# Second attention of a four-layer kernel: three SP transfers change place or queue, and the router's logits go in four parts

## The reference, cut to what matters

```
scores = einsum('bhqd,bhkd->bhqk', q, k) * scale, causal, + head_scales * geo
attn = softmax(scores);  out = einsum('bhqk,bhkd->bqhd', attn, v) @ w_out
x3 = layernorm(x2 + out)                 # x2: tokens before this layer
xn = rmsnorm(x3) * norm_weight
logits = xn @ router_weight.T + router_bias
probs = softmax(logits); gate_vals, expert_idx = top_k(probs, 2)
pos = rank of each choice within its expert; slot = min(pos, CAP - 1)
dispatch[e, slot] += xn;  experts run on dispatch;  results are gathered
```

## Time and profile before

| | us |
|---|---|
| time, median of 3 runs (1979.17 to 1983.17) | 1980.51 |
| time of the profiled execution | 1971.93 |
| its span | 1970.2 |
| mean granted clock | 0.945 |
| PE busy | 1813.4 (92%) |
| DVE busy | 1427.4 (72%) |
| ACT busy | 1123.9 (57%) |
| POOL busy | 504.8 (26%) |

### The profile page before, as it was taken

The page is one execution under the profiler, slowest core; times in us unless marked ns, Lnnn a source line. Parts: engine busy times, 40 slices in busy tenths (PEclk is TensorE's granted clock), DMA queues, the critical chain, the costliest instruction groups (busy, mean ns, idle before and its releaser), DMA issues. The chain is left out here.

```text
span 1970.2 us, 34757 instructions
## 1 busy us (share of the span) xinstructions
PE 1813.4 (92%) x12676; PEld 1183.6 (60%) x12676; DVE 1427.4 (72%) x2803; ACT 1123.9 (57%) x2228; POOL 504.8 (26%) x648
## 2 busy tenths in 40 slices
PE   8979999999999999799999889899897968899992
PEld 4545444444444444588888755555554457899992
DVE  7869999999999996467776465556564354566663
ACT  4635888888888889323222225454453523555554
POOL 5750000332000001222221122115142243244441
PEclk9976999999999999899999969989998989999996
DMA  4883734654354302115434466527463243556645
GB/s 168 289 239 46 116 82 93 142 137 127 62 82 71 63 19 81 41 51 176 138 107 128 153 164 145 127 65 192 99 168 85 72 160 109 134 142 146 157 91 184
DMA packets 169717, 238.99 MB, mean 121 GB/s; under 512 B 25689, under 2 KB 109178, under 8 KB 169568
## 3 DMA queue, kind: packets, MB, share of 16 engines
q1 hardware_dynamic: 138256, 178.82, 37.2%
q0 software_dynamic: 15200, 26.76, 5.8%
q10 hardware_dynamic: 16112, 31.46, 4.5%
HBM read 136.97 MB, written 96.60 MB: 119 GB/s over the span
## 5 line engine op out<-in xcount | busy, mean ns | idle before, releaser
L989 DVE TENSOR_REDUCE b_mx<-b_PM 128x1 f32<-128x512 f32 x1024 | 621.1, 681 | 22.3 <-PE b_PM L843 21.9
L965 ACT ACTIVATE b_probs<-b_PS 128x512 f32<-128x512 f32 x1000 | 523.9, 606 | 69.0 <-PE b_PS L897 53.7
L2784 ACT ACTIVATE d_probs<-d_PS 128x512 f32<-128x512 f32 (+3 forms) x384 | 167.0, 496 | 211.4 <-PE d_PS L2695 210.8
L843 PE MATMUL b_PM<-b_kst,b_qst 48*128 48x512 f32 x888 | 281.3, 431 | 0.0
L897 PE MATMUL b_PS<-b_qst,b_kst 50*128 50x512 f32 x744 | 256.8, 436 | 2.0 <-issue 0.2
L2824 DVE TENSOR_REDUCE d_mx<-d_PM 128x2 f32<-128x1024 f32 (+1 forms) x192 | 180.1, 950 | 97.4 <-PE d_PM L2647 66.0
L897 PEld LDWEIGHTS b_PS<-b_qst,b_kst 50*128 50x128 f32 x744 | 120.5, 184 | 163.3 <-ACT b_probs L965 147.5
L2747 POOL TENSOR_SCALAR_AFFINE_SELECT d_probs<-d_probs 128x128 f32<-128x128 f32 x256 | 73.8, 301 | 281.0 <-ACT d_probs L2784 276.4
L869 PE MATMUL b_PO<-b_probs,x_v 128*32 128x384 f32 (+2 forms) x2048 | 145.3, 390 | 0.0
L843 PEld LDWEIGHTS b_PM<-b_kst,b_qst 48*128 48x128 f32 x888 | 142.0, 184 | 5.1
L869 PE MATMUL b_PO<-b_probs,b_vst 128*32 128x384 f32 (+3 forms) x1960 | 143.0, 397 | 1.0 <-ACT b_probs L965 0.9
(11 more groups left out here) (300 smaller groups left out, 3762.4 us busy)
## 6 DMA issues: line engine op xcount, KB each, us to landing
halves<-a_parts SPq DMA_DIRECT2D x7, 2048.0 KB, 8.7
qk<-c_halves ACTq DMA_DIRECT2D x7, 2048.0 KB, 12.4
w_w<-L_ffn_fc1T SPq DMA_DIRECT2D x12, 1024.0 KB, 5.0
w_w<-L_ffn_fc2T SPq DMA_DIRECT2D x12, 1024.0 KB, 6.4
b_qst<-halves SPq DMA_DIRECT2D x72, 128.0 KB, 4.4
b_kst<-halves SPq DMA_DIRECT2D x72, 128.0 KB, 7.5
d_qst<-qk SPq DMA_DIRECT2D x36, 256.0 KB, 4.5
d_kst<-qk SPq DMA_DIRECT2D x36, 256.0 KB, 6.6
```

What stands on the lines that cost most here:

```text
L843: mm = pe.matmul(PM[n % MBANKS][:], qst[buf][at, p, first:first + P], kst[buf][at, p, kh * BLK:(kh + 1) * BLK], start=True, stop=True)
L965: act.activation(probs[:, s % RING], score_bank(g, s)[:], ACT.Exp).then_inc(exped, 1)
L989: dve.tensor_reduce(mx[:, half, (r * PAIRS0 + p) * TPH + t, kh:kh + 1], PM[n % MBANKS][:], AX.X, ALU.max)\
L2784: act.activation(probs[:, s % RING, 0:w], PS[bank(s)][:, 0:w], ACT.Exp).then_inc(exped, 1)
```

## The change

- `load_shares(g-1, 1)` stands ahead of `load(g+3)` on SP's queue instead of behind it. It does so in every group, so also in the first group of the next batch, which brings a batch's last shares.
- `load_tokens` and the `tokens.store` of batches 0 to 2 move from SP's queue to POOL's, to tick 4 of the same groups (T % 12 == 4, between POOL's masks of i = 3 and i = 8). POOL then waits for `x3_done` before it loads x2. The last two stores stay on SP and signal on a semaphore of their own.
- The logits of a full batch come in four parts of two token tiles each, at k = 27, 28, 29 and 30. Each part takes a place in the ring and has its own DVE scaling. The half batches at the end keep one part, at k = 30.
- All that follows the logits comes three ticks later: exponentials at 33, ranks at 42, scatter at 46 to 61. In the tail, where there is no attention, the order of the instructions stays the same.

```
-    LOGITS, EXPS, RANKS = 27, 30, 39
-    SCATTER = 43
+    LOGITS = (27, 28, 29, 30)
+    CHOICE = LOGITS[-1]
+    EXPS, RANKS = 33, 42
+    SCATTER = 46
...
+    def part_at(cls, u, k):
+        if k in cls.parts(u):
+            i, share = cls.parts(u).index(k), cls.UNITS[u][1] // len(cls.parts(u))
+            return i, range(i * share, (i + 1) * share), cls.parts_through(u - 1) + i + 1
...
             if b > 1:
-            sp.wait_ge(self.logits_ready, b - 1)
+            sp.wait_ge(self.logits_ready, self.parts_through(b - 2))
...
-    def load_tokens(self, sp, d, b):
+    def load_tokens(self, pool, d, b):
         if b > 0:
-            sp.wait_ge(self.x3_done, b * TPB)
+            pool.wait_ge(self.x3_done, b * TPB)
...
-        if k == self.LOGITS:
-            dve.wait_ge(self.logits_ready, u + 1)
+        if part := self.part_at(u, k):
+            i, ts, through = part
+            dve.wait_ge(self.logits_ready, through)
...
                 if g + 1 < GROUPS:
                     rows(g + 1)
+                if g > 0:
+                    route.load_shares(sp, d, g - 1, 1)
                 if g + BUFS - 1 < GROUPS:
                     if g > 0:
                         sp.wait_ge(pv_done, g * ROUNDS + RING // G1)
                     load(g + BUFS - 1)
-                if g > 0:
-                    route.load_shares(sp, d, g - 1, 1)
                 route.store_shares(sp, d, g, 0)
-                b = g // HG1
-                if g % HG1 == HG1 - 2:
-                    route.load_tokens(sp, d, b)
-                if g % HG1 == HG1 - 1 and b > 0:
-                    for n in range((b - 1) * HPS, b * HPS):
-                        tokens.store(sp, d, n)
...
+                if T < GROUPS * ROUNDS and T % ROUNDS == TPK:      # on POOL, behind mask(T)
+                    g = T // ROUNDS
+                    b = g // HG1
+                    if g % HG1 == HG1 - 2:
+                        route.load_tokens(pool, d, b)
+                    if g % HG1 == HG1 - 1 and b > 0:
+                        for n in range((b - 1) * HPS, b * HPS):
+                            tokens.store(pool, d, n, tokens.x3_out)
```

More of the change, by code:

```diff
@@ L1569, in __init__, with store @@
         self.x3 = a.sb("x3", [P, TILES, DIM])
-        self.x3_out = a.sem("x3_out")
+        self.x3_out, self.last_x3_out = a.sem("x3_out"), a.sem("last_x3_out")
         self.sums_in = [a.sem(f"sums_in{n}") for n in range(BLOCKS)]
-    def store(self, sp, d, n):
-        sp.dma_start(d["sums1"][n * BLK:(n + 1) * BLK, :].rearrange("(t p) c -> p t c", p=P),
-                     self.x3[:, n * TPK:(n + 1) * TPK]).then_inc(self.x3_out, 16)
+    def store(self, eng, d, n, out):
+        eng.dma_start(d["sums1"][n * BLK:(n + 1) * BLK, :].rearrange("(t p) c -> p t c", p=P),
+                      self.x3[:, n * TPK:(n + 1) * TPK]).then_inc(out, 16)
     def load_sums(self, sp, d, n):
@@ L1593 @@
     STEPS = 20
-    TICKS = 59
+    TICKS = 62
     WEIGH, WEIGH_LAST = (8, 12), (1,)
@@ L1610 @@
     LAST_POOL = dict(zip(range(SCATTER + BEHIND, SCATTER + BEHIND + 2 * TPK), zip(range(SCATTER, SCATTER + 2 * TPK))))
-    FILLS = {("project", 6): 26, ("project", 7): 24, ("logits", 3): 5, ("turn", 7): 8, ("logits", 4): 5}
+    FILLS = {("project", 6): 26, ("project", 7): 24, ("logits", 3, 0): 5, ("turn", 7): 8, ("logits", 4, 0): 5}
     LEAD = TPB // 2
@@ L1700, in entries, with parts, parts_through @@
     @classmethod
+    def parts(cls, u):
+        return cls.LOGITS if cls.UNITS[u][1] == TPB else cls.LOGITS[-1:]
+    @classmethod
+    def part_at(cls, u, k):
+        if k in cls.parts(u):
+            i, share = cls.parts(u).index(k), cls.UNITS[u][1] // len(cls.parts(u))
+            return i, range(i * share, (i + 1) * share), cls.parts_through(u - 1) + i + 1
+    @classmethod
+    def parts_through(cls, u):
+        return sum(len(cls.parts(i)) for i in range(u + 1))
+    @classmethod
     def entries(cls, u, k):
@@ L1706, in entries @@
                 found.append((name, n))
-        if k == cls.LOGITS:
-            found.append(("logits", u))
+        if part := cls.part_at(u, k):
+            found.append(("logits", u, part[0]))
         if k == cls.RANKS:
@@ L1772, in load_shares @@
         sp.dma_start(self.shares[b % 2][to % P:to % P + G1 * D1, half, to // P], share).then_inc(self.shares_in[half], 16)
-    def load_tokens(self, sp, d, b):
+    def load_tokens(self, pool, d, b):
         if b > 0:
-            sp.wait_ge(self.x3_done, b * TPB)
+            pool.wait_ge(self.x3_done, b * TPB)
         for i in range(HPS):
             tok = slice(b * SEQ + i * BLK, b * SEQ + (i + 1) * BLK)
-            sp.dma_start(self.x2[:, i], d["x2"][tok, :].rearrange("(t p) c -> p t c", p=P)).then_inc(self.x2_in[i], 16)
+            pool.dma_start(self.x2[:, i], d["x2"][tok, :].rearrange("(t p) c -> p t c", p=P)).then_inc(self.x2_in[i], 16)
     def wait_weights_free(self, sp, b):
         sp.wait_ge(self.projected, (b + 1) * HPS)
-        sp.wait_ge(self.logits_ready, b + 1 if b + 1 < BATCH else len(self.UNITS))
+        sp.wait_ge(self.logits_ready, self.parts_through(b if b + 1 < BATCH else len(self.UNITS) - 1))
     def fill(self, pe, ident, spare, *name):
@@ L1821, in multiply @@
             mm.then_inc(self.x3_turned, 1)
-        if k == self.LOGITS:
-            self.fill(pe, ident, spare, "logits", u)
-            out = self.bank("logits", u)
+        if part := self.part_at(u, k):
+            name = ("logits", u, part[0])
+            self.fill(pe, ident, spare, *name)
+            out = self.bank(*name)
             for n in self.blocks(u):
                 self.taken(pe, "turn", n)
-            self.free(pe, "logits", u)
-            for t in range(count):
+            self.free(pe, *name)
+            for t in part[1]:
                 i, at = (start + t) // TPK % HPS, (start + t) % TPK * P
@@ L1944, in choose @@
                .then_inc(self.xn_done, 1)
-        if k == self.LOGITS:
-            dve.wait_ge(self.logits_ready, u + 1)
[L1947 to L1950, removed]
+        if part := self.part_at(u, k):
+            i, ts, through = part
+            dve.wait_ge(self.logits_ready, through)
+            these = slice(lo + ts[0], lo + ts[-1] + 1)
+            dve.tensor_tensor(self.scaled[:, these],
+                              self.bank("logits", u, i)[:, 0, ts[0] * E:(ts[-1] + 1) * E].rearrange("p (t e) -> p t e", e=E),
+                              self.rroots[:, 1, these].unsqueeze(2).to_broadcast([P, len(ts), E]), ALU.mult)\
+               .then_inc(self.max_taken[self.entry["logits", u, i] % 2], 1)
+        if k == self.CHOICE + 1:
+            for i in range(len(self.parts(u))):
+                self.taken(dve, "logits", u, i)
             dve.tensor_tensor(self.logits[:, us], self.scaled[:, us], self.br[:].unsqueeze(1).to_broadcast([P, count, E]), ALU.add)\
@@ L1954, in choose @@
             dve.tensor_reduce(self.top[:, us], self.logits[:, us], AX.X, ALU.max).then_inc(step, 1)
-        if k == self.LOGITS + 2:
+        if k == self.CHOICE + 2:
             past(2)
@@ L1966, in choose @@
             dve.sem_inc(self.seen, 1)
-        for tile in self.tiles_at(u, k, self.LOGITS + 5):
+        for tile in self.tiles_at(u, k, self.CHOICE + 5):
             t = tile % TPB
@@ L1973, in choose @@
                 dve.sem_inc(self.seen, 1)
-        if k == self.LOGITS + 8:
+        if k == self.CHOICE + 8:
             for t in range(lo, lo + count // 2):
                 dve.max_index(self.besti[:, t], self.best[:, t], self.prob[:, t])
-        if k == self.LOGITS + 9:
+        if k == self.CHOICE + 9:
             for t in range(lo + count // 2, lo + count):
@@ L1984, in choose @@
         lead = self.SCAN_AT[u]
-        if k == self.LOGITS + 10:
+        if k == self.CHOICE + 10:
             past(9)
@@ L1993, in choose @@
                .then_inc(step, 1)
-        if k == self.LOGITS + 11:
+        if k == self.CHOICE + 11:
             for i in range(3):
@@ L2289, in gpsimd @@
         assert PLAIN * ST == MLPS
-        pool.wait_ge(tokens.x3_out, 16 * BLOCKS)
+        pool.wait_ge(tokens.x3_out, 16 * (BLOCKS - HPS))
+        pool.wait_ge(tokens.last_x3_out, 16 * HPS)
         for n in range(MLPS):
@@ L2623, in _ @@
                 sp.wait_ge(route.x3_done, (n + 1) * TPK)
-                tokens.store(sp, d, n)
+                tokens.store(sp, d, n, tokens.last_x3_out)
             route.wait_weights_free(sp, BATCH - 1)
```

4 lines of the change are left out of this document (2 added, 2 removed).

## The result

The changed kernel takes 1966.89 us (median of 9 runs, 1960.53 to 1970.71) against 1978.51 us (9 runs, 1974.21 to 1983.17) for the kernel before: ratio 0.9938, 95% interval 0.9922 to 0.9954. It is faster, by 12 us. The prediction said 1945.5 us, 35 us faster, with a range up to 1962. It had the sign and missed the size by a factor of three.

The account below looks back on a forecast made before the run. PE was taken to bound the second attention, with gains from its idle gaps and slow clock. 19.2 + 8.9 + 7.0 - 0.6 - 0.4 + 1.0 = 35 us, from the median of 1980.5 to 1945.5 us, with a range up to 1962.

Parts of the forecast that it names:

- the delay of the load behind the shares: SP's queue: the load comes one DMA issue of 0.58 us later, its buffers used more than a group later.
- Shares ahead of the load: Odd blocks' projections: three DVE waits go, 12.31 us, and the clock stays up, 6.91 us; together 19.2 us gained.
- Tokens on POOL: Waits for totals: PE gaps of 7.12 us and 4.2 us of slow clock go, less 2 x 1.20: 8.9 us gained.
- Logits: Logits in four parts: the slow clock behind units 0 and 2 goes; 7.0 us gained of at most 8.4.
- the banks: Logits: each part takes a bank, so the next tick's maximum waits for DVE; 0.2 us lost per unit, 0.6 in all.
- Choice three ticks later: DVE's small instructions meet other maxima and the ranks come to a short tick: a loss of 0.4 us in all.
- Tail: After x3 stores leave SP's queue the last shares can be earlier: between 0 and 2.2 us, taken as 1 gained.
- A: PE's clock falls elsewhere, behind small gaps or small products: 18 us not gained, 17 us faster, 1963.5 us; chance 0.12.
- B: Totals late all the same, token transfers sharing the 16 DMA engines: 8.9 us missing, 1954.5 us; chance 0.10.
- C: Token DMAs on POOL hold up the masks of round 8: 12 us slower at c = 8, 1992 us; chance 0.06.
- D: Shares land no earlier than DVE needs them because their own store lands late: 16 us left, 1964.5 us; chance 0.04.
- signs of being wrong: Batch periods between projections not falling some 12 us each, PEclk falling at new places, or DVE's wait for totals staying.

Follow-up runs that it names:

- the wide shares: Kernel before with its shares, still behind the large load, read by one DMA per head instead of one for two heads: 1961.92 us, ratio 0.9909.
- 15.3 in the second: The changed kernel run once more for a second profile, beside the kernel before at 1971.38 us: 1956.09 us, ratio 0.9921.
- the wide one: Changed kernel with the shares read by one DMA per head, run twice: 1936.51 us, ratio 0.9824, and 1956.26 us, ratio 0.9884.
- the wide kernel with later ranks: Changed kernel with shares by one DMA per head and ranks at k = 43 instead of 42: 1948.24 us, ratio 0.9842.
- the second and third series: Two series of four kernels, each on one chip beside the kernel before, at 1981.12 and 1979.43 us: ratios 0.9842 to 0.9946 and 0.9864 to 1.0002.
- the first series: Four kernels on one chip beside the kernel before at 1971.38 us: changed again, shares ahead in first groups only, wide shares, late weights; 0.9824 to 0.9921.

## Why the prediction missed the size

Two steps failed, the delay of the load behind the shares (put at nothing, 8.7 us) and the choice with its ranks (put at -0.4 us, measured -5.5). Both are read from the pair of traces.

*Shares ahead of the load.* The gain was forecast at 19.2 us and is 19.2 in this execution: the gaps at 1.33 to 1.47 us for 1.43, the projections at 3.72 us for 3.69. In several other executions with the shares in this place one or two of the three projections come at the slower clock (5.41 us), so it is in part luck that none did here. The first step that failed is the sentence behind it: "Behind the shares the load's eight instructions come one DMA issue of 0.58 us later; their buffers are used more than a group later." Both halves were wrong (and the instructions are seven). The load of group g + 3 goes out at about tick 8 of group g, and PE asks for its keys at tick 6 of group g + 1. In the trace after, `x_k` was issued from 1202.80 and PE stood for it until 1216.96, 14.2 us later. PE's wait began at 1214.33. Had each transfer landed in the 6.7 us of before, they would have been in time by some 4 us (by 4.8 for the first of the three, which are issued within a microsecond). That was all the slack. And the delay is not one issue but what the two-head DMA holds up behind it. This took 8.7 us in batch 0. No term of the sum asked what the shares' DMA costs by itself: its 10.66 us to land were read as "behind the load" alone. The trace of before had more to say. With no load ahead of it, the even half's DMA was issued at 1255.44 and DVE started on it at 1260.25, 4.8 us later, where a wide one lands in 2.1 us.

*Tokens on POOL.* 8.9 us forecast, 7.5 found here and 6.6 in the kernel with this part alone. The pair of direct DMAs was taken at 2 us on POOL and takes 1.5 to 1.6, and the masks of round 8 were not late. The mechanism was right, and a part of the same gain was to be had by the wide shares (8.6 us, with the stores where they were).

*Logits.* 7.0 forecast, less 0.6 for the banks, 7.7 in this trace, and nothing in the kernel with this part alone (-1.1), since the clock falls there in some executions with four parts too. That the sum's term looks right here is luck of one execution.

*Choice three ticks later.* This is the second step that failed: forecast as -0.4 us, the most mis-sized term. It gained 3.0 us at the choice and lost 8.5 at the ranks. The prediction had seen the place ("the ranks, for which PE waits, come to a short tick"), but bounded the loss by twice the 0.80 us that PE had idled before. A wait on a short tick has nothing to hide it. It was 2.12 us, and with the slow clock behind it (0.50 over 5.9 us in the second case) the two groups lost 3.6 and 5.0 us. The clock was priced for the gaps that went and not for the one that came.

*Tail.* 1 us forecast; 66.6 us before, 68.5, 67.1, 64.0 and 66.4 in the four traces without "issue" waits. Nothing that can be told from this.

*Rivals.* A (the clock falls elsewhere) was right in part: it did so behind the ranks, and behind a 1.33 to 1.47 us gap it fell in some executions (projection of 5.41 us) and not in others. B, C and D did not happen in the form given. B came nearest, with its transfers holding up small ones, but it had the wrong queue: what held them up was SP's own two-head DMA. Of the two losses that decided the size, late keys were on none of the lists, and the ranks only as a term of at most 1.6 us for each of two units. Of the prediction's own signs of being wrong two came: the clock fell at a new place (the ranks), and the two batch periods between the even projections fell by 17.7 us together instead of 24.

The sum by terms, 19.2 + 7.5 + 7.7 + 3.0 - 8.7 - 8.5, is 20 us. By medians the gain is 11.6 us in the first comparison and 15.3 in the second. The terms account for 20 us in one pair of traces, and the 5 to 8 us by which the medians are below it are not accounted for. They are no more than clock and tail vary between executions and chips (the ratio of one and the same kernel, the wide one, was 0.9824 on one chip and 0.9884 on another).

## What to carry to other kernels

Before a DMA is moved ahead of another in one queue, ask for its width as well as its bytes: the slowest dimension of both sides, and how long it takes to land where nothing is ahead of it. Follow the transfers that it passes to the first instruction that needs them, in ticks, and compare with their landing time. And when small instructions move to another tick, look at what stands in front of the one that an engine waits for: the same wait costs nothing behind eight products of 1.9 us in all, and some 4 us on a tick that has none.

The best version of the runs is the change with the shares read by one DMA per head: 0.9824 and 0.9884 on two chips, against 0.9921 for the change as it stands beside the first. (0.9847 and 0.9842, for the shares ahead in a first group only and for the wide kernel with later ranks, can't be told from it.) Cutting that one DMA in two, on the kernel before and with nothing else, gained about as much as the three parts together, if not more: 0.9909 [0.9880, 0.9937] against 0.9938 [0.9922, 0.9954] and 0.9921 [0.9894, 0.9948].

## What the runs showed of the hardware

- Behind a DMA of 128 KB whose slowest dimension is two, small DMAs in SP's queue took 5.01 and 8.10 us to issue and loads of 256 KB landed in 9.5 us (median). With it as two DMAs of 32 rows each, which landed in 2.1 us, they took 0.57 and 2.07 us, and 6.9.
- TensorE's clock fell behind a wait of 2.12 to 2.14 us for the ranks at both places in all eight traces that have it (the mean granted clock was 0.50 to 0.72 over the next 5 to 6 us), and behind one of 1.33 to 1.47 us in some. At the same place and with the same gap a projection took 3.72 us in one execution and 5.41 in another.
- PE stood in three to nine short waits with no releaser, the longest of a trace 0.43 to 2.25 us, behind the end of the second attention. They came in the first trace of the kernel after and in all eight of the second and third series, but not in the kernel before's nor in the four of the first series. The later weights load did not take them away.
